# Second self-attention with one combined query-key matrix instead of two projections

## The chip, the cores and the metric

The kernel runs on one core of one Trainium2 chip. The metric is the device time of the program in microseconds. A matmul of f32 operands is shown in the trace as two MATMUL records and two weight loads; a transpose on TensorE is one.

## The reference

A decoder of two layers works on x of 4 batches, 1024 rows and 256 features. Layer 0 is a masked self-attention of 16 heads, a cross-attention and a quantised feed-forward with a depthwise convolution. Layer 1 is the self-attention that is changed here, a cross-attention and a gated feed-forward. After each of the six parts the input is added and a layer norm follows. The part that is changed has a single head of 256 features:

```python
def _L1_attn_ref(x, W_query, W_key, W_value):
    q = jnp.einsum('bnd,de->bne', x, W_query)
    k = jnp.einsum('bnd,de->bne', x, W_key)
    v = jnp.einsum('bnd,de->bne', x, W_value)
    sqrt_d = jnp.sqrt(jnp.asarray(OUT_DIM, dtype=jnp.float32))
    scores = jnp.einsum('bie,bje->bij', q, k) / sqrt_d
    attn = jax.nn.softmax(scores, axis=1)
    return jnp.einsum('bij,bie->bje', attn, v)
```

The softmax runs over the query index i, and the result has one row for each key index j. There is no bias in q and k.

## The kernel before, in words

The program has four stages, one after the other. The third, from L1950 to L2556, computes three things interleaved: the rest of the quantised feed-forward of layer 0 (its first layer and convolution for batches 2 and 3, its second layer for all four), the self-attention of layer 1 for all four batches, and the first loads and projections of the fourth stage. The order is written out by hand in a loop over steps `s` (9 to 49) that stands once in each engine's block; each engine works its list in order and waits on semaphores. Eight steps make one batch. In the code `e` is the batch whose feed-forward is finished, `m` is the place in its eight steps, and tile `s - 17` is the tile of 128 keys whose scores are made in step `s`.

- TensorE, of one step with both kinds of work: the scores of a tile (`scores`, L2083: 128 keys by 1024 queries into psA), a chunk of the first feed-forward layer (`first_layer`, L2072), the values of the tile before (`values`, L2094), and the transposes of the exponentials (`transpose_rows`, L2103).
- At `m` = 5 the second feed-forward layer (`second_layer`, L2119, eight tiles of 8 matmuls). At `m` = 6 the rows of the batch are transposed (`transpose_x`, L2124, four groups), and keys and queries of the first 512 rows are projected (`project_qk`, L2132: for each two chunks of 128 output features, each chunk two matmuls of 512 columns). At `m` = 7 keys and queries of the last 512 rows, and the first four tiles of `v` (`project_v`, L2139). The other four tiles of `v` come in the step after it. For batch 1 the transposes for the next first layer (`prepare`, L2065) follow at the end of the step `m` = 6.
- ScalarE copies every projection out of PSUM (`copy_xt` L2257, `copy_qk` L2264, `copy_v` L2271). Beside that it has the exponentials of the scores (L2235) and, for the feed-forward, Silu, Abs and two taps of the convolution.
- VectorE finds the maximum of each key tile's scores (L2448), adds the middle tap, rounds the hidden values (`hq`, L2488) and does residuals and norms. GpSimd adds the last tap (L2339), scales the hidden values (L2349) and rounds x for the next first layer (L2331, L2332).

All projections, `v` tiles, `values` and second-layer tiles share the two banks of psO in turn: `slot_c` (L2037) makes TensorE wait until the result before last has been read. `xt`, the transposed exponentials and some small spreads share the two banks of psB in the same way (`slot_t`, L2031). `number_c` fixes the turn of each result ahead. `XT3` holds the transposed rows of one batch, `ka` the keys of one batch, `qa` the queries of two. The trace calls `XT3` XT_sb, `wk_a1` wk_a_sb and `wq_a1` wq_a_sb.

Of the kernel before, what the change touches and what calls it, by code (L numbers as in the profile page):

```python
# [22 lines left out]
F32 = mybir.dt.float32  # L23
# [23 lines left out]
def decoder_kernel(nc, t, out):  # L47
# [21 lines left out]
    def sb(name, shape, dt=F32, ctx=top, side="left"):  # L69
        return ctx.enter_context(nc.sbuf_tensor(name + "_sb", shape, dt, side=side))  # L70
# [1478 lines left out]
    XR = sb("XR", [P, 2, NT, D], F32, third_stage)  # L1549
    XT3 = sb("XT3", [P, KC, S], F32, third_stage)  # L1550
    xq = sb("xq", [P, NT, D], BF16, f0_stage, "right")
# [7 lines left out]
    hq = sb("hq", [P, FH, S], BF16, f0_stage, "right")  # L1559
    qa = sb("qa", [P, 2, KC, S], F32, third_stage)  # L1560
    ka = sb("ka", [P, KC, S], F32, third_stage)
# [75 lines left out]
    for s in range(BEGIN, STEPS + 1):  # L1637
# [18 lines left out]
        if m in (6, 7) and e is not None:  # L1656
            if m == 6:
                for i in range(NT // 2):
                    number_t(("xt", e, i))
            for qk in ("k", "q"):  # L1660
                for c in range(KC):
                    number_c((qk, e, c, m - 6))
        if m == 7 and e is not None:
# [286 lines left out]
    with nc.Block() as block:  # L1950
        @block.sync
        def _(sp):
# [28 lines left out]
            load_xr(0)  # L1981
            for dst, name in ((wk_a1, "L1_attn_W_key"), (wq_a1, "L1_attn_W_query"), (wv_a1, "L1_attn_W_value")):
                sp.dma_start(dst[:, :, :], feature_rows(t[name])).then_inc(wa_loaded, 16)
# [46 lines left out]
        def _(pe):  # L2030
# [52 lines left out]
            def scores(a):  # L2083
                b, j = a // NT, a % NT
                if j == 0:
                    pe.wait_ge(c_act, C_FREED[("q", b, KC - 1, 1)])
                if a > 0:
                    pe.wait_ge(s_exped, a)
                for n in range(NC):
                    last = gemm(psA[:, 0, n * 512:(n + 1) * 512], lambda k: ka[:, k, j * P:(j + 1) * P],  # L2090
                                lambda k: qa[:, b % 2, k, n * 512:(n + 1) * 512], KC)
                last.then_inc(s_full, 1)
# [38 lines left out]

            def project_qk(qk, e, c, n):  # L2132
                w = wk_a1 if qk == "k" else wq_a1
                pe.wait_ge(t_act, T_FREED[("xt", e, 2 * n + 1)])
                k = slot_c((qk, e, c, n))
                gemm(psO[:, k, :], lambda i: w[:, i, c * P:(c + 1) * P], lambda i: XT3[:, i, n * 512:(n + 1) * 512],
                     KC).then_inc(c_full, 1)

            def project_v(e, j):  # L2139
                pe.wait_ge(t_act, T_FREED[("xt", e, j // 2)])  # L2140
                k = slot_c(("v", e, j))
                gemm(psO[:, k, 0:D], lambda i: XT3[:, i, j * P:(j + 1) * P], lambda i: wv_a1[:, i, :],
                     KC).then_inc(c_full, 1)
# [3 lines left out]
            for s in range(BEGIN, STEPS + 1):  # L2147
# [24 lines left out]
                if m in (6, 7) and e is not None:  # L2172
                    if m == 6 and e == 0:
                        pe.wait_ge(wa_loaded, 16 * 3)
                    if m == 6:
                        for i in range(NT // 2):
                            transpose_x(e, i)
                    for qk in ("k", "q"):
                        for c in range(KC):
                            project_qk(qk, e, c, m - 6)  # L2180
                if m == 7 and e is not None:
# [17 lines left out]
        def _(act):  # L2199
# [57 lines left out]
            def copy_xt(e, i):  # L2257
                key = ("xt", e, i)
                act.wait_ge(t_full, T_SLOT[key])
                nc.scalar.activation(XT3[:, :, 2 * i * P:2 * (i + 1) * P].rearrange("p c (n q) -> p n c q", n=2),  # L2260
                                     psB[:, t_bank(key), :].rearrange("p (n c q) -> p n c q", n=2, c=KC),
                                     ACT.Copy).then_inc(t_act, 1)
# [15 lines left out]
            for s in range(BEGIN, STEPS + 1):  # L2278
# [17 lines left out]
                if m in (6, 7) and e is not None:  # L2296
                    if m == 6:
                        for i in range(NT // 2):
                            copy_xt(e, i)
                    for qk in ("k", "q"):  # L2300
                        for c in range(KC):
                            copy_qk(qk, e, c, m - 6)
                if m == 7 and e is not None:
# [738 lines left out]
```

## Time and profile before

| | us |
|---|---|
| median of 3 runs | 2462.32 |
| lowest and highest run | 2461.2, 2466.6 |
| span of the profiled execution | 2470.6 |
| TensorE busy in the span | 2108.0 |
| VectorE, ScalarE, GpSimd busy | 1446.1, 1215.5, 767.3 |
| third stage in the profiled execution, about | 1521 to 2000 |

No time other than its span is given for the profiled execution; the span is 8.3 us above the median of the runs. An instruction's duration in the trace is longer than its share of the engine when instructions follow each other closely: eight records of a 128x512 f32 matmul are listed with 3.60 us, while the next group starts 3.43 us after them. The cost of a group on TensorE is therefore read from start to start.

### The profile page before, as it was taken

The page shows a single profiled execution, that of the slowest core. Times are in us where ns is not written, and L with a number is a line of the kernel's source. Part 1 is how long each engine was busy: PE and PEld are TensorE (multiplying, and loading weights), DVE is VectorE, ACT ScalarE, POOL GpSimd, SP SyncE. Part 2 cuts the span into 40 slices and gives each one's busy share as a digit, 9 for nine tenths or more (in the row PEclk, how much of TensorE's full clock was granted, in tenths as well). Part 3 has the DMA queues.
Part 4 walks back from the last instruction along what each step waited for, and adds up shares of the span by engine and source line. Part 5 has one row for each costly group of instructions (what it writes and reads, how often), then busy time and mean ns, then how long its engine had stood idle before and what let it go on. Part 6 is the DMA issues. An engine that isn't in the chain of part 4 may idle for free. (4 is left out here: it accounts for less than half of the span.)

```text
span 2470.6 us, 33295 instructions
## 1 busy us (share of the span) xinstructions
PE 2108.0 (85%) x11586; PEld 1180.7 (48%) x11586; DVE 1446.1 (59%) x2698; ACT 1215.5 (49%) x2773; POOL 767.3 (31%) x1082
## 2 busy tenths in 40 slices
PE   6778888888888869999999985889899977788886
PEld 3333344344343345565555554556566643445455
DVE  5565466455655146566787885494834344557555
ACT  2345534544444436565787771567642314354352
POOL 4250220221001020011454551384824222443333
PEclk8889999999999879999999998999999978899898
DMA  7425433343241020000110114010001156544321
GB/s 157 105 45 135 83 75 70 75 86 76 42 67 45 20 74 1 7 29 25 44 59 24 47 46 156 32 43 9 28 26 49 37 118 123 116 94 89 80 59 40
DMA packets 132520, 156.60 MB, mean 63 GB/s; under 512 B 36493, under 2 KB 102929, under 8 KB 132258
## 3 DMA queue, kind: packets, MB, share of 16 engines
q1 hardware_dynamic: 132354, 154.47, 26.2%
q8 instruction: 94, 1.54, 0.3%
q14 instruction: 72, 0.59, 0.1%
HBM read 107.55 MB, written 46.86 MB: 62 GB/s over the span
## 5 line engine op out<-in xcount | busy, mean ns | idle before, releaser
L530 ACT ACTIVATE pbuf_sb<-psB 128x512 f32<-128x512 f32 (+1 forms) x608 | 330.8, 573 | 343.5 <-PE psB L409 318.5
L716 DVE TENSOR_REDUCE negm_sb<-psA 128x1 f32<-128x768 f32 (+6 forms) x352 | 347.4, 1022 | 135.6 <-PE psA L397 132.9
L406 PE MATMUL psB<-qst_sb,kst_sb 99*128 99x512 bf16 (+3 forms) x768 | 237.0, 339 | 42.0 <-ACT pbuf_sb L530 34.1
L1257 ACT ACTIVATE pw_sb<-psA,nmx_sb 128x154 f32<-128x154 f32 x512 | 191.9, 389 | 133.5 <-DVE nmx_sb L1402 133.5
L395 PE MATMUL psA<-kst_sb,qst_sb 96*128 96x512 bf16 (+3 forms) x768 | 200.0, 339 | 40.9 <-DVE negm_sb L716 34.4
L423 PE MATMUL psO<-pbuf_sb,V_sb 128*32 128x512 f32 (+3 forms) x1536 | 170.3, 517 | 8.4 <-ACT OT_sb L516 7.1
L1402 DVE TENSOR_REDUCE nmx_sb<-psA 128x4 f32<-128x616 f32 x128 | 101.8, 796 | 125.3 <-PE psA L1026 125.0
L406 PEld LDWEIGHTS psB<-qst_sb,kst_sb 99*128 99x128 bf16 x768 | 75.2, 99 | 183.2 <-ACT pbuf_sb L530 145.9
L2801 ACT ACTIVATE pb_sb<-psB 128x512 f32<-128x512 f32 x160 | 92.8, 601 | 134.3 <-PE psB L2691 131.1
L2918 DVE TENSOR_REDUCE negm_sb<-psA 128x2 f32<-128x320 f32 x256 | 115.9, 480 | 70.8 <-PE psA L2681 66.1
L395 PEld LDWEIGHTS psA<-kst_sb,qst_sb 96*128 96x128 bf16 x768 | 60.9, 99 | 165.0 <-DVE negm_sb L716 100.7
L2681 PE MATMUL psA<-kst_sb,qst_sb 97*128 97x160 bf16 x512 | 83.2, 250 | 46.3 <-DVE negm_sb L2918 40.6
L2448 DVE TENSOR_REDUCE nma_sb<-psA 128x1 f32<-128x1024 f32 x32 | 39.1, 1222 | 140.8 <-PE psA L2045 140.8
L979 PE MATMUL psO<-XT_sb,wq_x_sb 128*128 128x512 f32 x256 | 121.4, 597 | 0.0
L567 POOL TENSOR_TENSOR OT_sb<-OT_sb,rden_sb 128x1024 f32<-128x1024 f32 x15 | 35.3, 2352 | 277.0 <-DMA rden_sb<-dens_dram 277.0
L979 PE MATMUL psO<-wo_x_sb,ox_sb 128*128 128x256 f32 x512 | 115.6, 379 | 1.7 <-DVE famw_sb L1488 0.9
L2045 PE MATMUL psO<-va_sb,pat_sb 128*128 128x256 f32 x512 | 115.9, 379 | 1.0 <-DVE pat_sb L2475 1.0
L2045 PE MATMUL psA<-qa_sb,ka_sb 128*128 128x512 f32 x256 | 116.7, 599 | 0.0
L553 POOL TENSOR_TENSOR q_sb<-q_sb,parts_sb 128x512 f32<-128x512 f32 x32 | 37.8, 1180 | 229.7 <-ACT parts_sb L510 229.4
L2045 PEld LDWEIGHTS psO<-va_sb,pat_sb 128*128 128x128 f32 x512 | 96.9, 190 | 22.6 <-issue 7.7
L397 PE MATMUL psA<-masku_sb,identb_sb 128*128 128x128 bf16 x512 | 107.6, 224 | 0.0
L1040 PE MATMUL psB<-ident_sb,pr_sb 128*128 128x128 f32 x512 | 83.6, 286 | 27.0 <-DVE pt_sb L1395 26.9
(308 smaller groups left out, 4580.6 us busy)
## 6 DMA issues: line engine op xcount, KB each, us to landing
qst_sb<-parts_dram SPq DMA_DIRECT2D x192, 128.0 KB, 4.6
rden_sb<-dens_dram SPq DMA_DIRECT2D x128, 128.0 KB, 2.7
parts_dram<-parts_sb SPq DMA_DIRECT2D x32, 384.0 KB, 2.8
kst_sb<-parts_dram SPq DMA_DIRECT2D x96, 128.0 KB, 7.3
x_dram<-X_sb SPq DMA_DIRECT2D x64, 128.0 KB, 1.7
y_dram<-yw_sb SPq DMA_DIRECT2D x16, 512.0 KB, 2.8
Y_sb<-y_dram SPq DMA_DIRECT2D x16, 512.0 KB, 9.3
parts_dram<-partsb_sb SPq DMA_DIRECT2D x16, 384.0 KB, 3.0
```

Source lines behind the costliest of these rows:

```text
L395: nc.tensor.matmul(psA[:, k, at + lo:at + hi], qst[0:QK_ROWS, gg % 3, h, j * P:(j + 1) * P], kst[0:QK_ROWS, gg % 3, h, lo:hi], start=True, ...
L397: last = nc.tensor.matmul(psA[:, k, at + w - P:at + w], identb[:, :], masku[:, :], start=False, stop=True)
L406: last = nc.tensor.matmul(psB[:, k, at:at + hi - lo], kst[0:MAX_ROWS, gg % 3, h, i * P:(i + 1) * P], qst[0:MAX_ROWS, gg % 3, h, lo:hi], st ...
L423: last = nc.tensor.matmul(psO[32 * h:32 * h + 32, c, lo - c * 512:hi - c * 512], V[:, b % 2, i, at:at + 32], pbuf[:, i % 2, h, lo:hi], sta ...
L530: nc.scalar.activation(pbuf[:, key % 2, heads[0]:heads[-1] + 1, lo:hi], psB[:, (nb.n - 1) % 2, 0:len(heads) * (hi - lo)] .rearrange("p (h ...
L716: nc.vector.tensor_reduce(out=negm[:, gg % 2, heads[0]:heads[-1] + 1, j], in_=psA[:, (na.n - 1) % 2, :].rearrange("p (h n) -> p h n", h=le ...
L979: last = nc.tensor.matmul(dst, lhsT(i), rhs(i), start=(i == 0), stop=(i == n - 1))
L1257: last = nc.scalar.activation(pw[:, m % 2, h, :], psA[:, m % 2, at:at + K], ACT.Exp, bias=nmx[:, m % 2, h:h + 1], accum_out=psx[:, m % 3, ...
L1402: nc.vector.tensor_reduce(out=nmx[:, m % 2, :].rearrange("p (b a) -> p a b", a=2), in_=psA[:, m % 2, :].rearrange("p (a n) -> p a n", a=2) ...
L2045: last = nc.tensor.matmul(dst, lhsT(i), rhs(i), start=(i == 0), stop=(i == n - 1))
L2801: nc.scalar.activation(pb1[:, v % 2, h, :], psB[:, (nb.n - 1) % 2, :], ACT.Exp).then_inc(b_free, 1)
L2918: nc.vector.tensor_reduce(out=negm1[:, gg % 2, 2 * half:2 * half + 2, j], in_=psA[:, 0, half * 512:half * 512 + 2 * KP].rearrange("p (a n) ...
```

## The change

The query and key weights are loaded transposed. Their product, 256 by 256, is made once, before the rows of batch 0 are transposed, and ScalarE copies it to `wqk` with the factor 1/16 (`D ** -0.5`). For each batch only one projection is made with it (`project_k`), and the scores multiply its result by the plain transposed rows `XT3`, which is now kept for two batches. `qa`, its projection and its copies are gone. Loads, with their sizes and their order, stay; only the names of the two arrays change.

```diff
-    XT3 = sb("XT3", [P, KC, S], F32, third_stage)
+    XT3 = sb("XT3", [P, 2, KC, S], F32, third_stage)
+    wqk = sb("wqk", [P, KC, D], F32, third_stage)
-    qa = sb("qa", [P, 2, KC, S], F32, third_stage)
...
-            for qk in ("k", "q"):
-                for c in range(KC):
-                    number_c((qk, e, c, m - 6))
+            if m == 6 and e == 0:
+                number_c(("wqk",))
+            for c in range(KC):
+                number_c(("k", e, c, m - 6))
...
             def scores(a):
...
-                    pe.wait_ge(c_act, C_FREED[("q", b, KC - 1, 1)])
+                    pe.wait_ge(c_act, C_FREED[("k", b, KC - 1, 1)])
...
-                                lambda k: qa[:, b % 2, k, n * 512:(n + 1) * 512], KC)
+                                lambda k: XT3[:, b % 2, k, n * 512:(n + 1) * 512], KC)
...
-            def project_qk(qk, e, c, n):
-                w = wk_a1 if qk == "k" else wq_a1
+            def combine_weights():
+                k = slot_c(("wqk",))
+                for c in range(KC):
+                    last = gemm(psO[:, k, c * D:(c + 1) * D], lambda i: wk_a1[:, i, c * P:(c + 1) * P], lambda i: wq_a1[:, i, :], KC)
+                last.then_inc(c_full, 1)
+
+            def project_k(e, c, n):
                 pe.wait_ge(t_act, T_FREED[("xt", e, 2 * n + 1)])
-                k = slot_c((qk, e, c, n))
-                gemm(psO[:, k, :], lambda i: w[:, i, c * P:(c + 1) * P], lambda i: XT3[:, i, n * 512:(n + 1) * 512],
+                pe.wait_ge(c_act, C_FREED[("wqk",)])
+                k = slot_c(("k", e, c, n))
+                gemm(psO[:, k, :], lambda i: wqk[:, i, c * P:(c + 1) * P], lambda i: XT3[:, e % 2, i, n * 512:(n + 1) * 512],
                      KC).then_inc(c_full, 1)
...
                     if m == 6 and e == 0:
                         pe.wait_ge(wa_loaded, 16 * 3)
+                        combine_weights()
...
-            def copy_qk(qk, e, c, n):
-                key = (qk, e, c, n)
+            def copy_weights():
+                key = ("wqk",)
                 act.wait_ge(c_full, C_SLOT[key])
-                dst = ka[:, c, n * 512:(n + 1) * 512] if qk == "k" else qa[:, e % 2, c, n * 512:(n + 1) * 512]
-                nc.scalar.activation(dst, psO[:, c_bank(key), :], ACT.Copy,
-                                     scale=1.0 if qk == "k" else D ** -0.5).then_inc(c_act, 1)
+                nc.scalar.activation(wqk[:, :, :].rearrange("p c n -> p (c n)"), psO[:, c_bank(key), :], ACT.Copy,
+                                     scale=D ** -0.5).then_inc(c_act, 1)
+
+            def copy_k(e, c, n):
+                key = ("k", e, c, n)
+                act.wait_ge(c_full, C_SLOT[key])
+                nc.scalar.activation(ka[:, c, n * 512:(n + 1) * 512], psO[:, c_bank(key), :], ACT.Copy).then_inc(c_act, 1)
```

On TensorE, at the start of the third stage's attention (batch 0, from the second feed-forward layer to the first scores), the order before is this; x4 here counts matmuls as the program issues them.

```order
L2045 MATMUL psO<-w2q_sb,hq_sb 128x256 x64
L2128 MATMUL psB<-ident_sb,XR_sb 128x128 x16
L2045 MATMUL psO<-XT_sb,wk_a_sb 128x512 x4
L2045 MATMUL psO<-XT_sb,wq_a_sb 128x512 x4
L2045 MATMUL psA<-xqT_sb,w1q_sb 128x512 x4
L2045 MATMUL psO<-XT_sb,wk_a_sb 128x512 x4
L2045 MATMUL psO<-XT_sb,wq_a_sb 128x512 x4
L2045 MATMUL psO<-wv_a_sb,XT_sb 128x256 x8
L2045 MATMUL psA<-qa_sb,ka_sb 128x512 x4
```

And this is the order of the change at the same place, where wqk_sb is the product of the two weights.

```order
L2046 MATMUL psO<-w2q_sb,hq_sb 128x256 x64
L2046 MATMUL psO<-wq_a_sb,wk_a_sb 128x256 x4
L2129 MATMUL psB<-ident_sb,XR_sb 128x128 x16
L2046 MATMUL psO<-XT_sb,wqk_sb 128x512 x4
L2046 MATMUL psA<-xqT_sb,w1q_sb 128x512 x4
L2046 MATMUL psO<-XT_sb,wqk_sb 128x512 x4
L2046 MATMUL psO<-wv_a_sb,XT_sb 128x256 x8
L2046 MATMUL psA<-XT_sb,ka_sb 128x512 x4
```

Both query projections are gone; four shorter matmuls stand between the second layer and the transposes of x.

On TensorE at batch 1, `m` = 6, where the transposes of the rounded rows (xq_sb) follow the projections, the order before is:

```order
L2128 MATMUL psB<-ident_sb,XR_sb 128x128 x16
L2045 MATMUL psO<-XT_sb,wk_a_sb 128x512 x4
L2045 MATMUL psO<-XT_sb,wq_a_sb 128x512 x4
L2053 MATMUL psB<-identb_sb,xq_sb 128x128 x16
L2061 MATMUL psB<-ident_sb,finvx_sb 128x128 x8
L2045 MATMUL psA<-qa_sb,ka_sb 128x512 x4
```

In the change it is:

```order
L2129 MATMUL psB<-ident_sb,XR_sb 128x128 x16
L2046 MATMUL psO<-XT_sb,wqk_sb 128x512 x4
L2054 MATMUL psB<-identb_sb,xq_sb 128x128 x16
L2062 MATMUL psB<-ident_sb,finvx_sb 128x128 x8
L2046 MATMUL psA<-XT_sb,ka_sb 128x512 x4
```

The transposes of xq_sb now come right behind the key projection.

## Rows read from the trace of the kernel before

**Rows 1.** Page: busy time of each engine in the whole span.
```profile
PE 2108.0 (85%) x11586; PEld 1180.7 (48%) x11586; DVE 1446.1 (59%) x2698; ACT 1215.5 (49%) x2773; POOL 767.3 (31%) x1082
```

**Rows 2.** Stretches: busy us by engine, TensorE clock granted, DMA share, GB/s.
```profile
core 0: us, PE busy (x) PEld busy (x) DVE busy (x) ACT busy (x) POOL busy (x), PEclk, DMA share, GB/s
1553.00:1576.50 23.50, 20.85 (x60) 10.40 (x59) 3.91 (x7) 9.25 (x16) 4.03 (x7) 0.93 0.00 0
1600.00:1650.00 50.00, 43.56 (x190) 28.16 (x190) 42.16 (x61) 39.11 (x41) 47.38 (x63) 0.93 0.16 50
1789.00:1996.00 207.00, 201.89 (x846) 136.28 (x845) 80.95 (x176) 68.94 (x115) 64.53 (x112) 1.00 0.16 43
```

**Rows 3.** Waits, 1550 to 2000 us: total us, times, longest.
```profile
DVE nma_sb L2448 <- PE psA L2045: 140.8, 23, 14.8
ACT pa_sb L2235 <- DVE nma_sb L2448: 105.2, 22, 13.8
```

**Rows 4.** Instructions of L2045: count, ns min/median/max, first and last start.
```profile
L2045 PE MATMUL psO<-XT_sb,wq_a_sb x64: 592/592/667, 1560.9 to 1910.8; 128*128 128x512 f32 x64
```

**Rows 5.** TensorE in order of time, batch 3: start us, length, group.
```profile
1893.19 3.60 PE L2045 MATMUL psO<-XT_sb,wq_a_sb 128*128 128x512 f32 x8
1896.62 3.60 PE L2045 MATMUL psA<-qa_sb,ka_sb 128*128 128x512 f32 x8
```

**Rows 6.** TensorE in order of time, batch 0, projections.
```profile
1555.29 0.66 PE L2128 MATMUL psB<-ident_sb,XR_sb 128*128 128x128 f32 x4 [1.89 <-DVE XR_sb L2509]
1555.78 5.29 PE L2045 MATMUL psO<-XT_sb,wk_a_sb 128*128 128x512 f32 x8
1560.91 3.60 PE L2045 MATMUL psO<-XT_sb,wq_a_sb 128*128 128x512 f32 x8
1564.35 1.03 PE L2045 MATMUL psA<-xqT_sb,w1q_sb 128*128 128x512 bf16 x4
1569.57 3.67 PE L2045 MATMUL psO<-XT_sb,wq_a_sb 128*128 128x512 f32 x8 [0.77 <-ACT ka_sb L2268]
1576.69 3.60 PE L2045 MATMUL psA<-qa_sb,ka_sb 128*128 128x512 f32 x8
```

**Rows 7.** VectorE and ScalarE, batch 0: residual of tile 6, first copy of x.
```profile
1551.24 0.48 DVE L2501 SCALAR_TENSOR_TENSOR XR_sb<-psO,finvy_sb,XR_sb 128x256 f32<-128x256 f32 x1
1552.00 1.09 ACT L2260 ACTIVATE XT_sb<-psB 128x512 f32<-128x512 f32 x2 [26.66 <-PE psB L2128]
```

**Rows 8.** TensorE, batch 1: v of 128x256 columns, then scores.
```profile
1695.11 3.77 PE L2045 MATMUL psO<-wv_a_sb,XT_sb 128*128 128x256 f32 x16
1698.71 3.60 PE L2045 MATMUL psA<-qa_sb,ka_sb 128*128 128x512 f32 x8
```

**Rows 9.** TensorE, batch 1, m = 6.
```profile
1672.38 3.60 PE L2045 MATMUL psO<-XT_sb,wq_a_sb 128*128 128x512 f32 x8
1675.81 1.06 PE L2053 MATMUL psB<-identb_sb,xq_sb 128*128 128x128 bf16 x16
1677.73 2.05 PE L2061 MATMUL psB<-ident_sb,finvx_sb 128*128 128x128 f32 x16 [0.86 <-ACT xqT_sb L2206]
1679.61 3.60 PE L2045 MATMUL psA<-qa_sb,ka_sb 128*128 128x512 f32 x8
```

**Rows 10.** GpSimd and ScalarE at the same place.
```profile
1673.02 0.85 POOL L2332 TENSOR_SCALAR xq_sb<-Xq_sb 128x256 bf16<-128x256 f32 x1
1676.50 2.06 ACT L2206 ACTIVATE xqT_sb<-psB 128x512 bf16<-128x512 bf16 x4
```

**Rows 11.** TensorE, batch 0: second-layer wait, scores after a wait.
```profile
1597.52 2.05 PE L2061 MATMUL psB<-ident_sb,fscy_sb 128*128 128x128 f32 x16 [1.04 <-DVE pat_sb L2475]
1626.80 1.26 PE L2107 MATMUL psB<-ident_sb,pa_sb 128*128 128x128 f32 x8 [2.23 <-ACT pa_sb L2235]
1627.85 5.17 PE L2045 MATMUL psA<-qa_sb,ka_sb 128*128 128x512 f32 x8
1632.86 1.03 PE L2045 MATMUL psA<-xqT_sb,w1q_sb 128*128 128x512 bf16 x4
1641.22 3.58 PE L2045 MATMUL psO<-w2q_sb,hq_sb 128*128 128x256 bf16 x16 [1.93 <-DVE hq_sb L2488]
```

**Rows 12.** GpSimd, batch 0 to 1: scaling of the hidden values, first and last of three groups.
```profile
1602.19 8.29 POOL L2349 TENSOR_TENSOR Y_sb<-Y_sb,rb_sb 128x256 f32<-128x256 f32 x12
1633.41 7.02 POOL L2349 TENSOR_TENSOR Y_sb<-Y_sb,rb_sb 128x256 f32<-128x256 f32 x8
```

More of the change, by code:

```diff
@@ L1981, in _ @@
             load_xr(0)
-            for dst, name in ((wk_a1, "L1_attn_W_key"), (wq_a1, "L1_attn_W_query"), (wv_a1, "L1_attn_W_value")):
+            for dst, name in ((wk_a1, "L1_attn_W_keyT"), (wq_a1, "L1_attn_W_queryT"), (wv_a1, "L1_attn_W_value")):
                 sp.dma_start(dst[:, :, :], feature_rows(t[name])).then_inc(wa_loaded, 16)
@@ L2141, in project_v @@
                 k = slot_c(("v", e, j))
-                gemm(psO[:, k, 0:D], lambda i: XT3[:, i, j * P:(j + 1) * P], lambda i: wv_a1[:, i, :],
+                gemm(psO[:, k, 0:D], lambda i: XT3[:, e % 2, i, j * P:(j + 1) * P], lambda i: wv_a1[:, i, :],
                      KC).then_inc(c_full, 1)
@@ L2177, in _ @@
                             transpose_x(e, i)
-                    for qk in ("k", "q"):
-                        for c in range(KC):
-                            project_qk(qk, e, c, m - 6)
+                    for c in range(KC):
+                        project_k(e, c, m - 6)
                 if m == 7 and e is not None:
@@ L2259, in copy_xt @@
                 act.wait_ge(t_full, T_SLOT[key])
-                nc.scalar.activation(XT3[:, :, 2 * i * P:2 * (i + 1) * P].rearrange("p c (n q) -> p n c q", n=2),
+                nc.scalar.activation(XT3[:, e % 2, :, 2 * i * P:2 * (i + 1) * P].rearrange("p c (n q) -> p n c q", n=2),
                                      psB[:, t_bank(key), :].rearrange("p (n c q) -> p n c q", n=2, c=KC),
                                      ACT.Copy).then_inc(t_act, 1)
-            def copy_qk(qk, e, c, n):
-                key = (qk, e, c, n)
+            def copy_weights():
+                key = ("wqk",)
                 act.wait_ge(c_full, C_SLOT[key])
-                dst = ka[:, c, n * 512:(n + 1) * 512] if qk == "k" else qa[:, e % 2, c, n * 512:(n + 1) * 512]
-                nc.scalar.activation(dst, psO[:, c_bank(key), :], ACT.Copy,
-                                     scale=1.0 if qk == "k" else D ** -0.5).then_inc(c_act, 1)
+                nc.scalar.activation(wqk[:, :, :].rearrange("p c n -> p (c n)"), psO[:, c_bank(key), :], ACT.Copy,
[4 more added lines that the diff above has]
+                nc.scalar.activation(ka[:, c, n * 512:(n + 1) * 512], psO[:, c_bank(key), :], ACT.Copy).then_inc(c_act, 1)
             def copy_v(e, j):
@@ L2296, in _ @@
                 if m in (6, 7) and e is not None:
+                    if m == 6 and e == 0:
+                        copy_weights()
                     if m == 6:
@@ L2299, in _ @@
                             copy_xt(e, i)
-                    for qk in ("k", "q"):
-                        for c in range(KC):
-                            copy_qk(qk, e, c, m - 6)
+                    for c in range(KC):
+                        copy_k(e, c, m - 6)
                 if m == 7 and e is not None:
@@ L3022 @@
         if name in ("L0_attn_w_in", "L0_attn_w_out", "L0_xattn_Wq", "L0_xattn_Wk", "L0_xattn_Wv", "L0_xattn_Wo",
-                    "L0_ffn_w1", "L0_ffn_w2", "L1_ffn_W_r", "L1_ffn_W_k", "L1_ffn_W_v"):
+                    "L0_ffn_w1", "L0_ffn_w2", "L1_ffn_W_r", "L1_ffn_W_k", "L1_ffn_W_v", "L1_attn_W_query", "L1_attn_W_key"):
             arrays[name + "T"] = np.ascontiguousarray(a.T)
```

## The prediction

> **What bounds the kernel now.** I read the page's busy times first, then the stretches, then the waits, then the engines in order of time around every projection. Over the whole span TensorE is the busiest engine by far, 2108.0 of 2470.6 us [rows 1]. That is an average over four stages, so the third stage is read by itself. From 1789 to 1996 us, where the projections of batches 2 and 3 lie, TensorE is busy 201.89 of 207 us at full granted clock; no other engine reaches 81 us [rows 2]. Around batch 0's and 1's feed-forward it is less clear: from 1600 to 1650 us TensorE is busy 43.56 of 50 us, GpSimd 47.38 and VectorE 42.16. The waits say who is late: the longest total is VectorE's wait for scores from TensorE, 140.8 us in 23 waits, and behind it ScalarE's wait for the maxima of those scores, 105.2 us [rows 3]. So TensorE work that stands ahead of scores delays them, except where another engine's chain reaches the same point later. The prediction is a walk over the eight places where a query projection stands, asking at each what TensorE finds when it comes 3.43 us earlier.
>
> **What goes.** 64 records of a 128x512 f32 matmul read the query weights [rows 4]: 4 batches x 2 halves of the rows x 4 matmuls x 2 records. In batch 3 eight of them start at 1893.19 and the scores behind them at 1896.62, so one group costs 3.43 us [rows 5], and eight groups 8 x 3.43 = 27.4 us. The 16 copies on ScalarE go too; I count them at nothing, since in 1789 to 1996 us ScalarE is busy 68.94 of 207 us.
>
> **What comes.** The product of the weights is four matmuls of 256 columns, eight records. Sixteen such records take 1698.71 - 1695.11 = 3.60 us with the waits for their copies [rows 8], so eight take 1.8. They stand after the second layer of batch 0 and before the transposes of x, where TensorE later sits idle 1.89 us until VectorE has normalised the last rows [rows 6]. The product's bank is that of the second layer's tile 6, which VectorE reads at 1551.24 to 1551.72 [rows 7]. So it runs from about 1551.8 to 1553.5. The first eight transposes of x then run about 1553.5 to 1554.4. ScalarE, which starts the x copies at 1552.00 today and needs 0.55 us for each [rows 7], first copies the product, about 1553.7 to 1554.3, then the first two groups until about 1555.4. The last transposes, which start at 1555.29 today, need the second of these copies (same bank), so they start about 1555.4, and the key projection about 1555.9 instead of 1555.78. That is 0.15 us lost: the cover is the 1.89 us wait. If there were no cover, the price would be the 1.8 us and one copy of 0.6, 2.4 in all. The new wait of `project_k` on the copy of the product is met at about 1554.3, before the rows are ready, and is free in all later batches. The loads of the weights are the same in size and place, and the wait for them was already there.
>
> **Batch 0, first half, and the clock.** The key projection of this half takes 1560.91 - 1555.78 = 5.13 us, not 3.43 [rows 6]; the granted clock in this stretch is 0.93 [rows 2], so part of the group ran at 1.2 GHz and the rest at 2.4. Before it fell TensorE had stood idle 1.89 us with a few short transposes around. With the change this gap is filled by the product. Bounds for the effect: nothing (5.13 stays), or 5.13 - 3.43 = 1.7 us gained. I take 1.7, since the activity before the fall is what the change adds to; the other end stays in the range.
>
> The Trainium skill, "TensorE: Matmul & The Clock Gate", part 1, says that the throttled clock is the default and that activity of TensorE releases it, while idle time brings it back. By that rule the filled gap gains the 1.7 us; without it the sum would be 1.7 us smaller. The same rule speaks against the change elsewhere, since it makes TensorE less busy; this is the last rival below.
>
> **Batch 0, second half.** TensorE waits 0.77 us for the copy of the first key chunk, because ScalarE is in the convolution taps [rows 6]. After the change it is the first `v` tile that needs this same bank, at the same distance from the first-layer group that releases the taps. So the wait stays at 0.77 us and the full 3.43 us go. Batch 0 gives 2 x 3.43 - 0.15 + 1.7 = 8.4 us, seen as first scores at about 1568.3 instead of 1576.69 [rows 6].
>
> **Batch 1, first half.** Here something else is late next. The transposes of xq follow the projections, at 1675.81 [rows 9], and the last xq tile is ready on GpSimd at 1673.02 + 0.85 = 1673.87 [rows 10]. With the query group gone TensorE comes at 1672.38. The first eight transposes (tiles 0 to 3) run at once, the last eight wait until 1673.9 and end about 1674.4. ScalarE copies each half in 1.03 us (2.06 for both [rows 10]); the second half's copy ends about 1675.6, and the last spread group, about 0.9 us long, can start only then. Scores start about 1676.5 instead of 1679.61: 3.1 us gained, 0.3 lost. If GpSimd were later by a microsecond relative to TensorE, a microsecond more would be lost, so I bound this place by 1 and 3.43.
>
> **The other places.** Batch 1, second half: 3.43. Batch 2 and 3, both halves: TensorE goes from the projection to scores or to `v` without any idle time [rows 2, 5], and the two copies left end before the next user of their bank, as they do now: 4 x 3.43 = 13.7.
>
> **Later work** moves as a whole. The GpSimd chain that ends in the rounding for which TensorE waits 1.93 us at 1641.22 starts behind the scale spreads of TensorE at 1597.52 [rows 11, 12], so it comes earlier with them. The fourth stage's loads are issued ahead of batch 3's projections; 6.9 us less stand between them and their first use.
>
> **Sum.** 8.4 + 3.1 + 3.43 + 13.7 = 28.6 us. The profiled span would go from 2470.6 to 2442.0. The runs' median is 8.3 us below that span, so the gain is taken from the median: 2462.3 - 28.6 = 2433.7 us. Own bounds: at best everything, 27.4 + 1.7 = 29.1; at worst no clock gain, an uncovered product (2.4) and 1 us only at batch 1: 27.4 - 2.4 - 2.4 = 22.6. With some 2 us for the spread of the runs (2461.2 to 2466.6), and one more at the low end for a fall of the clock elsewhere that may vanish, that is 2430 to 2442.
>
> **Rivals.**
> 1. The GpSimd chain takes the gain of the first two batches. From 1600 to 1650 us GpSimd is 95% busy [rows 2], and the scaling runs from 1602.19 to 1640.43 with other work between [rows 12]. If its start were set by data or by its own queue, and not by the spreads, the 8.4 and 6.5 us of batches 0 and 1 would turn into longer waits at 1641.22 and its counterpart. Left are 13.7 us: 2448.6. Against it: the scaling reads the spread scales that TensorE makes at 1597.52, and those stand behind batch 0's projections in TensorE's own order.
> 2. Copies become late. With half as many matmuls between results, each of the eight halves could meet the 0.77 us wait that one shows now [rows 6]: 7 x 0.77 = 5.4 us less, 2439. Against it: `v` tiles come only after both key chunks, and a chunk takes 1.7 us against a copy of 0.6.
> 3. Slower: the clock. After an idle of 2.23 us the scores at 1627.85 took 5.01 us to the next group instead of 3.43 [rows 11], 1.58 us for one fall to 1.2 GHz. TensorE loses 27 us of dense work in this stage and keeps its waits, so such falls could become more frequent. They decide from 28.6 / 1.58 = 18 further falls on; 22 would make it 6 us slower, 2468. Against it: the stretch where half of the removed groups lie has clock 1.00 and stays without gaps.
>
> By the rule on the clock gate in the Trainium skill, named above, more idle time lowers the clock; the trace agrees for the fall at 1627.85, 1.58 us.
>
> **Chances.** Forecast (2430 to 2437) 0.70; the copies or a later GpSimd at batch 1 (2437 to 2443) 0.14; the GpSimd chain (2443 to 2455) 0.08; nothing gained, by a mixture that I can't name 0.03; slower by the clock 0.05. The first two hold 0.84, so the range is 2430 to 2442. A difference under 0.2%, 4.9 us, can't be told from none. Faster 0.92, same 0.03, slower 0.05.
>
> **What would show it.** No records of the query group, 64 fewer, and eight new ones of 128x256 at the start. First scores of batch 0 about 8.4 us earlier, at 1568.3, and the key group there with 3.4 to 3.6 us (right on the clock) or about 5.1 (wrong). At batch 1 a wait of about 1 us of the xq transposes for xq_sb. Batches 2 and 3 shorter by 6.9 us each with no new wait. VectorE's total wait for scores smaller by some 27 us. It would be wrong if TensorE's waits for hq_sb (1.93 us) grew by several microseconds, if waits for ka_sb stood before each `v` group, or if the granted clock of the stage's second half fell below 1.00.

## The result, and the profile after

| | before | changed |
|---|---|---|
| median of the first comparison, us | 2463.55 (2461.2 to 2466.6, 4 runs) | 2445.99 (2445.07 to 2447.15, 4 runs) |
| ratio, 95% interval | | 0.9924 (0.991 to 0.9938) |
| all executions of the study: mean and its standard error | 2468.1, 0.6 (93 runs) | 2445.2, 1.2 (13 runs) |
| all executions: median, lowest, highest | 2467.5, 2450.9, 2481.2 | 2445.4, 2436.9, 2452.3 |
| span of the first profile | 2470.6 | 2445.4 |

The changed kernel is 17.6 us faster in the first comparison, where 28.6 were forecast and a time of 2430 to 2442 us. Over all executions, which were taken on several occasions and chips, it is 22.9 +- 1.3 us faster. So the direction was right and the size was not. The third stage gave what was forecast, as the next part shows. Of the shortfall about half comes from which executions of the kernel before were compared, and about half was lost outside the third stage.

The 93 executions leave out one, e3, which is told of below. `+-` is one standard error throughout, worked out as if the executions were independent.

Page of the changed kernel, busy time of each engine; it answers to [rows 1]:

```profile
PE 2085.8 (85%) x11503; PEld 1174.1 (48%) x11530; DVE 1449.0 (59%) x2698; ACT 1206.4 (49%) x2758; POOL 767.8 (31%) x1082
```

TensorE is listed with 22.3 us less, and its share of the span is unchanged. The program has 56 matmul records fewer (64 gone, 8 new), as the weight loads show (11586 to 11530); the page lists 83 fewer, so some 27 records are missing from this trace and the busy time is only roughly comparable.

**The third stage.** TensorE in order of time, changed kernel, batch 0; it answers to [rows 6, 7]. Columns: start, length, group, and in brackets the idle time ahead and who ended it.

```profile
1554.49 1.96 PE L2046 MATMUL psO<-wq_a_sb,wk_a_sb 128*128 128x256 f32 x8 [0.34 <-DVE XR_sb L2513]
1556.29 1.04 PE L2129 MATMUL psB<-ident_sb,XR_sb 128*128 128x128 f32 x8
1557.72 1.12 PE L2129 MATMUL psB<-ident_sb,XR_sb 128*128 128x128 f32 x8 [0.39 <-ACT XT_sb L2267]
1558.67 3.60 PE L2046 MATMUL psO<-XT_sb,wqk_sb 128*128 128x512 f32 x8
...
1562.97 3.60 PE L2046 MATMUL psO<-XT_sb,wqk_sb 128*128 128x512 f32 x8
1567.34 3.69 PE L2046 MATMUL psO<-wv_a_sb,XT_sb 128*128 128x256 f32 x16 [0.77 <-ACT ka_sb L2280]
1570.87 3.60 PE L2046 MATMUL psA<-XT_sb,ka_sb 128*128 128x512 f32 x8
```

The product starts at 1554.49 and the transposes that had waited 1.89 us now wait 0.39 us, for a copy. The key group is listed with 3.60 us where it had 5.29 before. From start to start it took 5.13 before and 3.66 now (1558.67 to 1562.33); here the first of four records of the next group is missing, and the profiles that have it give 3.44. The wait of 0.77 us for the key copy is there, ahead of `v`. First scores come 27.70 us after the first second-layer matmul (1543.17 to 1570.87), where they came 36.28 after it before (1540.41 to 1576.69): 8.6 us, predicted 8.4.

Batch 1, first half, TensorE; it answers to [rows 9]:

```profile
1663.52 3.90 PE L2046 MATMUL psO<-XT_sb,wqk_sb 128*128 128x512 f32 x8
1667.25 0.61 PE L2054 MATMUL psB<-identb_sb,xq_sb 128*128 128x128 bf16 x8
1668.19 0.62 PE L2054 MATMUL psB<-identb_sb,xq_sb 128*128 128x128 bf16 x8 [0.33 <-POOL xq_sb L2344]
1669.17 2.05 PE L2062 MATMUL psB<-ident_sb,finvx_sb 128*128 128x128 f32 x16 [0.36 <-ACT xqT_sb L2213]
1671.06 3.60 PE L2046 MATMUL psA<-XT_sb,ka_sb 128*128 128x512 f32 x8
```

And GpSimd at the same place, answering to [rows 10]:

```profile
1667.29 0.85 POOL L2344 TENSOR_SCALAR xq_sb<-Xq_sb 128x256 bf16<-128x256 f32 x1
```

The last eight transposes wait 0.33 us for the xq tile that ends at 1668.14. From the key group to the scores before, 10.67 us; now 7.54: 3.13 gained, predicted 3.1. That the two agree so closely is in part luck: the xq tile was ready 4.62 us after the start of the key group and not 4.93 as before, and from there to the scores it took 2.92 us and not the 2.6 of the forecast.

Batch 3, TensorE, second half of the projections; it answers to [rows 5]:

```profile
1882.12 3.60 PE L2046 MATMUL psO<-XT_sb,wqk_sb 128*128 128x512 f32 x8
1885.55 3.77 PE L2046 MATMUL psO<-wv_a_sb,XT_sb 128*128 128x256 f32 x16
1889.16 3.60 PE L2046 MATMUL psA<-XT_sb,ka_sb 128*128 128x512 f32 x8
```

And stretches of the changed kernel, answering to [rows 2] (the same parts of the program for the second and third row there), with the fourth stage:

```profile
core 0: us, PE busy (x) PEld busy (x) DVE busy (x) ACT busy (x) POOL busy (x), PEclk, DMA share, GB/s
1777.00:1970.00 193.00, 187.88 (x812) 129.97 (x811) 80.93 (x176) 64.18 (x107) 64.49 (x112) 1.00 0.17 47
1594.00:1640.00 46.00, 38.64 (x161) 25.16 (x162) 38.23 (x50) 36.40 (x39) 44.82 (x56) 0.93 0.17 55
1976.00:2445.00 469.00, 378.78 (x1888) 215.34 (x1888) 262.62 (x655) 185.62 (x333) 169.14 (x277) 0.89 0.42 90
```

The stretch without gaps is 14 us shorter for the same work but the projections (193 against 207), still at clock 1.00. Waits of the changed kernel, 1550 to 1974 us; they answer to [rows 3]:

```profile
DVE nma_sb L2460 <- PE psA L2046: 117.3, 23, 12.0
ACT pa_sb L2242 <- DVE nma_sb L2460: 105.2, 22, 13.8
```

VectorE's wait for scores fell by 23.5 us (some 27 were forecast); ScalarE's wait behind it is the same 105.2. Two of the prediction's signs of being wrong are read from TensorE's own waits in the same stretch. Before, for the rounded hidden values:

```profile
PE psO L2045 <- DVE hq_sb L2488: 3.8, 2, 1.9
```

In the changed kernel, for them and for the key copies:

```profile
PE psO L2046 <- DVE hq_sb L2500: 3.8, 2, 1.9
PE psO L2046 <- ACT ka_sb L2280: 0.8, 1, 0.8
```

The waits for hq_sb did not grow, and of the waits for ka_sb there is only the one.

The gain place by place, from the start times of the same groups in both profiles:

| place | gained, us | predicted |
|---|---|---|
| batch 0, both halves and the clock | 8.58 | 8.4 |
| batch 1, first half | 3.13 | 3.1 |
| batch 1, second half | 3.44 | 3.43 |
| batches 2 and 3, four halves | 3.43, 3.44, 3.42, 3.44 | 4 x 3.43 |
| between them | -0.4 | 0 |
| third stage | 28.45 | 28.6 |

The 0.4 us are lost just ahead of batch 1's key projection, and there the clock is lower: from 1655 to 1670 us of the changed kernel the granted clock is 0.77, at the same place before (1661 to 1676) 0.89.

**The rest.** From the first scores of the fourth stage on, before took 2470.6 - 2001.87 = 468.7 us and the changed kernel 2445.4 - 1976.18 = 469.2. Ahead of the first second-layer matmul they took 1540.4 and 1543.2. These two parts, which no edit touches, are where the rest of the story is.

### The profile page after: what moved, and what is told of

Its sections match the earlier page's. It is cut to its first block and busy times, and to the rows that moved or that the text cites. A ratio compares the mean times of both kernels' runs of the same rounds, so it can differ in the third digit from the quotient of the medians.

```text
span 2445.4 us, 33126 instructions
## 1 busy us (share of the span) xinstructions
PE 2085.8 (85%) x11503; PEld 1174.1 (48%) x11530; DVE 1449.0 (59%) x2698; ACT 1206.4 (49%) x2758; POOL 767.8 (31%) x1082
## 5 line engine op out<-in xcount | busy, mean ns | idle before, releaser
L2046 PE MATMUL psA<-XT_sb,ka_sb 128*128 128x512 f32 x256 | 116.0, 596 | 0.0
L1040 PE MATMUL psB<-ident_sb,pr_sb 128*128 128x128 f32 x512 | 83.6, 286 | 27.1 <-DVE pt_sb L1395 26.9
```

The source lines that it names most:

```text
L2046: last = nc.tensor.matmul(dst, lhsT(i), rhs(i), start=(i == 0), stop=(i == n - 1))
```

## The experiments

All the profiles of the study are cut in the same three parts: the time until the first matmul of the second layer (L2122), from there to the first scores of the fourth stage (here the third stage), and the rest. "First scores" is their distance from the first second-layer matmul.

| profile | first part | third stage | fourth | first scores |
|---|---|---|---|---|
| before | 1540.4 | 461.5 | 468.7 | 36.3 |
| e1, before | 1531.9 | 463.1 | 466.8 | 36.2 |
| e13, before | 1539.0 | 461.7 | 472.0 | 36.3 |
| e14, before | 1538.9 | 463.0 | 470.2 | 36.2 |
| e10, before, other arrays | 1539.0 | 461.4 | 468.6 | 36.2 |
| e9, before with the product | 1536.7 | 460.9 | 472.6 | 34.8 |
| changed | 1543.2 | 433.0 | 469.2 | 27.7 |
| e2, changed | 1537.7 | 433.1 | 472.8 | 27.8 |
| e4, changed | 1543.7 | 433.0 | 472.9 | 27.7 |
| e15, changed | 1536.5 | 432.8 | 470.0 | 27.8 |
| e16, changed | 1536.7 | 432.4 | 472.0 | 27.3 |
| e8, changed without the product | 1543.3 | 434.4 | 471.8 | 29.2 |
| e5, e6, e7, changed with a delay | 1549.9, 1542.5, 1540.6 | 433.5, 434.5, 435.2 | 469.1, 465.3, 471.1 | 27.6, 27.8, 27.8 |
| e11, projections twice, batches 0, 1 | 1542.7 | 445.0 | 467.8 | 33.7 |
| e12, projections twice, batches 2, 3 | 1537.1 | 446.7 | 466.6 | 27.8 |

### Both kernels again (e1 to e4, e13 to e16)

Edit: none. The question was why the profiles were 25 us apart and the timed runs 17.6.

> The kernel before, unchanged, run again to see how its executions spread and where the profiled one lay. Theory A (the profiled execution of before was an unusually long one, its span of 2470.6 us stands 7 to 9 us above its other runs): spans here lie near 2462 us, and the new profile shows where the 8 us of difference were: in the granted clock of stages 1, 2 or 4 or in the third stage. Theory B (the four runs of before happened to be short): spans here spread from 2460 to 2471 and the median is nearer to 2468.

> The changed kernel, unchanged, timed in more rounds. Theory A: ratio again 0.991 to 0.994, time 2446 us. Theory B: the ratio moves to about 0.9885, a gain of 28 us, since the third stage alone is 28 us shorter in the two profiles at hand.

> The kernel before once more, for a third profile. Theory A: span near 2462 us, the third stage from its first second-layer matmul to the first scores of the fourth stage shorter than the 461.5 us of the first profile, or the other stages shorter by 8 us. Theory B: span anywhere from 2460 to 2471.

> The changed kernel once more, for a third profile. Both theories: span 2443 to 2446 us; the third stage from its first second-layer matmul to the first scores of the fourth stage 433 us as in the first profile, if the third stage hardly varies.

Measured: e1 2471.15 us median (2463.09 to 2479.5, 12 runs) against 2467.52 for 17 further runs of the same kernel, ratio 1.0012 (0.9996 to 1.0028). e2 2444.54 (2436.91 to 2452.31, 6 runs), ratio 0.9907 (0.9886 to 0.9927). e4 2451.35. e3 had a mean granted clock of 0.729 and took 2830.9 us; even in its third stage (1757 to 2309 us), where the first two profiles come to 0.97, it was 0.75. Neither theory had it, and nothing is read of the change from it.

Theory A falls: the profiled execution of before was not unusual. Before spreads from 2451 to 2481 us, and the four runs of the first comparison lay 4.6 us under the mean of all 93. Theory B is right in kind, but hardly in size: the ratio went to 0.9907, which is 23 us, and its interval, 18 to 28 us, just misses B's 0.9885. e4's span of 2449.6 us lay above the 2443 to 2446 expected, its third stage at the expected 433.0. So 6 us were still missing: 29.2 in the third stage (means 462.1 and 432.9 of five profiles each, e10 counted as before), 22.9 +- 1.3 in all. This sets a difference of ten profiles against one of 106 executions, and the profiled ones need not be typical.

One place of spread is seen by laying e1 beside the first profile. TensorE, before, first stage, at the key tile behind the first maxima:

```profile
177.40 0.82 PE L395 MATMUL psA<-kst_sb,qst_sb 96*128 96x512 bf16 x2 [10.45 <-DVE negm_sb L716]
```

The same instruction in e1:

```profile
166.03 0.82 PE L395 MATMUL psA<-kst_sb,qst_sb 96*128 96x512 bf16 x2 [4.42 <-DVE negm_sb L716]
```

The wait is 4.4 to 4.8 us in some executions and 8.3 to 10.6 in the others (10.07 in the first profile of the changed kernel), for one and the same program; e3 is left out. It was short in 2 of 6 profiles of before (e9, e10 counted) and in 2 of 11 of the others. It doesn't fix the length of the first part by itself: e10 has a short one (4.51) and a first part of 1539.0 us, e15 a long one (10.56) and 1536.5.

Is the missing 6 us chance? With e13 to e16 more profiles were taken.

> Another profile of the kernel before. Over all its executions so far the changed kernel is 22.3 us shorter, though its third stage is 28.4 shorter in every profile; 6 us are lost outside the third stage. Theory I (a wait of TensorE in the first stage, 4.4 or about 10 us long, and the fourth stage's length, 466 to 473 us, fall out by chance, and fell worse for the changed kernel in both): first second-layer matmul 1532 to 1544 us, fourth stage 466 to 473, no difference in the means of the two kernels over more profiles. Theory J (the changed kernel really is later): before starts the second layer at 1532 to 1540, the changed kernel at 1540 to 1545.

> As for the run before it: one more profile of the kernel before. Theory J has its first second-layer matmul at or before 1540 us and its fourth stage at 467 to 469 us, theory I at any value between 1532 and 1550, and 466 to 473.

> One more profile of the changed kernel. Third stage 433.0 us again. Theory J: first second-layer matmul 1540 us or later and a fourth stage of 469 to 473 us; theory I: any value between 1532 and 1550, and 465 to 473.

> As for the run before it: third stage 433.0 us; by theory J the first second-layer matmul at 1540 us or later and 469 to 473 us for the fourth stage, by theory I any value.

Measured: 2474.42, 2473.95, 2441.07 and 2442.84 us. Theory J falls in its sharp form: the changed kernel's first part ended at 1536.5 and 1536.7 us, under the 1540 that it required, and the fourth stages of e13 and e14, 472.0 and 470.2, lie above the 467 to 469 that it required of before. The means of five profiles each are 1537.8 and 1539.6 for the first part, 469.3 and 471.4 for the fourth stage. That is 1.7 and 2.1 us more for the changed kernel, each from values that scatter over 4 to 9 us, so chance is not excluded for either. The 6.3 +- 1.4 us are more than chance; that the profiles locate 3.8 of them in these two parts is an indication and no more. The other 2.5 are not in the profiles at all: by their spans the two kernels are 25.5 us apart (2469.2 and 2443.8 in the mean of five).

**The clock of the timed executions.** Each execution is recorded with its span and mean granted clock, except the four timed runs of before in the first comparison. In every profile but e3's the granted clock is 0.5 (1.2 GHz) or 1 (2.4 GHz) at any time, so twice its shortfall from 1, times the span, is the time at 1.2 GHz. From these rows:

| executions | number | mean granted clock | at 1.2 GHz, us | time, us |
|---|---|---|---|---|
| before | 89 | 0.9483 | 255.1 +- 1.6 | 2468.3 |
| before with the product (e9), with other arrays (e10) | 24 | 0.9482 | 255.2 +- 2.3 | 2467.1 |
| changed, projections twice (e11, e12) | 20 | 0.9467 | 261.2 +- 3.4 | 2454.6 |
| changed with a delay (e5 to e7) | 33 | 0.9461 | 263.8 +- 2.3 | 2447.3 |
| changed | 13 | 0.9455 | 266.1 +- 2.9 | 2445.2 |

The changed kernel spends 11.1 +- 3.3 us more at 1.2 GHz. The same holds on each occasion by itself: in the executions taken together with e1 to e4 it is 270.2 against 259.4 us, and with e5 to e7 263.8 against 253.3. Nor is it arithmetic: 28.6 us less at full clock alone would leave the mean at 0.9477. Among the 89 executions of before, each further microsecond at 1.2 GHz goes with 0.37 us of time, and 255.1 and 266.1 us then differ by 4.1 us. At the same time at 1.2 GHz the changed kernel is 27.1 +- 0.9 us faster. So about 4 of the missing 6 us go together with more time at the lower clock. Whether the clock makes the time or a longer wait makes both is not shown, and where it happens isn't either: the five profiles of the changed kernel have 261 us at 1.2 GHz in the mean, those of before 265.

### A delay ahead of the fourth stage (e5 to e7)

```diff
             def normalise(a):
                 dve.wait_ge(arstd_ready, a + 1)
+                if a == NT * B - 1:
+                    for _ in range(1):   # 2 in e6, 3 in e7
+                        link(nc.vector.tensor_copy(XT3[:, 0, 1, :], XT3[:, 0, 0, :]))
```

> The changed kernel with one VectorE copy of 1024 elements (about 0.7 us) put between the last norm's wait and the last norm of the third stage, so that the fourth stage starts 0.7 us later after the same third stage. Theory C (what the fourth stage takes depends on where its start falls against the rhythm in which the granted clock changes; the changed kernel's three profiles all start it at one such place and take 469.2, 472.8, 472.9 us from the first scores on, those of before start at two others and take 468.7 and 466.8): the fourth stage changes by 1 to 5 us for a delay of 0.7, downwards if it meets the places of before. Theory D (the fourth stage's time has nothing to do with its start; the changed program has it longer by 3 us for its code or data placement, or by chance): fourth stage 469 to 473 us as without the delay, total 0.7 us longer.

> The same with two such copies, about 1.4 us. Theory C: the fourth stage again another length, between 466 and 473 us, always the same one in the profile and other stretches of 1.2 GHz than without the delay. Theory D: 469 to 473 us, total 1.4 us longer.

> The same with three such copies, about 2.2 us. Theory C: near the second profile of before, whose fourth stage took 466.8 us, so 466 to 468 us and a total not above the changed kernel's 2445.9. Theory D: 469 to 473 us, total 2.2 us longer.

Measured: 2446.55 us (2438.61 to 2454.81, 12 runs), 2448.84 (2443.68 to 2451.73, 9 runs) and 2447.77 (2438.95 to 2457.93, 12 runs); ratios 0.9909, 0.9930, 0.9925. Fourth stages 469.1, 465.3 and 471.1 us. Neither theory came out clean: e5 doesn't tell them apart, since its 469.1 lies in the range of D and also below two of the three lengths without a delay by 4 us; e6 fits neither; e7 misses the 466 to 468 of C and fits D. The delays changed the third stage by 0.5, 1.5 and 2.2 us, and the totals by 0.6 to 2.9, as a mere delay would. But the fourth stage of the changed kernel without any delay takes 469.2 to 472.9, and the delayed ones reach 465.3, below any of before, so a long fourth stage is no fixed property of the changed program. The fourth stage of e6 as one stretch; columns: start and end, length, busy time and instructions of each engine, granted clock, DMA share and what was moved in GB/s:

```profile
1977.00:2442.00 465.00, 375.90 (x1888) 214.08 (x1888) 262.45 (x655) 185.42 (x333) 169.13 (x277) 0.89 0.42 91
```

The same stretch of the program in e2, the changed kernel without a delay:

```profile
1971.00:2443.00 472.00, 378.25 (x1888) 215.12 (x1886) 263.27 (x655) 185.91 (x333) 168.77 (x277) 0.89 0.42 89
```

TensorE is busy 375.90 us of 465 and 378.25 us of 472, at the same mean clock to two digits, 0.89. So of the 7 us between them 2.35 are busy time and 4.65 are waiting (89.1 against 93.75 us). What selects the one or the other length was not found and stays open.

### Without the product, and the product alone (e8, e9)

```diff
                         pe.wait_ge(wa_loaded, 16 * 3)
-                        combine_weights()
...
-                gemm(psO[:, k, :], lambda i: wqk[:, i, c * P:(c + 1) * P], ...
+                gemm(psO[:, k, :], lambda i: wk_a1[:, i, c * P:(c + 1) * P], ...
```

Without the product its copy, its turn of the psO banks and the waits for it are gone too.

> The changed kernel without the product of the weights: keys are projected with the key weights as loaded, so the scores are not those of the reference; nothing else differs. If the product's only effects are those of the prediction (0.15 us lost behind the 1.89 us wait, 1.7 us won because the clock stays at 2.4 GHz): the key group of batch 0 takes about 5.1 us again, and first scores come about 1.5 us later after the first second-layer matmul than the 27.7 us of the changed kernel, 29.2 us. If the clock's better place in the changed kernel has another cause, the key group stays at 3.4 us and first scores come at 27.5 us.

TensorE, e8, the key group of batch 0 and the transposes ahead of it:

```profile
1558.11 0.72 PE L2127 MATMUL psB<-ident_sb,XR_sb 128*128 128x128 f32 x4 [1.89 <-DVE XR_sb L2515]
1558.63 5.26 PE L2044 MATMUL psO<-XT_sb,wk_a_sb 128*128 128x512 f32 x8
1563.73 1.03 PE L2044 MATMUL psA<-xqT_sb,w1q_sb 128*128 128x512 bf16 x4
```

The wait of 1.89 us is back, the key group takes 5.10 us, and first scores come at 29.2 us, as the sum had it. From 1558 to 1565 us the granted clock of e8 is 0.76, from 1558 to 1563 us of the changed kernel 1.00. One execution, 2451.27 us.

e9 adds the same product and its copy to the kernel before, used by nothing:

```diff
                     if m == 6 and e == 0:
                         pe.wait_ge(wa_loaded, 16 * 3)
+                        combine_weights()
```

> The kernel before with the product of the weights and its copy added, and used by nothing; both projections stay. If the product costs nothing behind the 1.89 us wait and keeps the clock at 2.4 GHz, the key group of batch 0 takes 3.4 us instead of 5.1, first scores come 34.8 us after the first second-layer matmul instead of 36.3, and the third stage is 460.0 instead of 461.5 us; the total 1 to 2 us under before, within its uncertainty. If the product costs its 1.8 us and its copy, the third stage is 463 us.

TensorE, e9, batch 0:

```profile
1548.18 1.97 PE L2048 MATMUL psO<-wq_a_sb,wk_a_sb 128*128 128x256 f32 x8 [0.34 <-DVE XR_sb L2519]
...
1552.37 3.60 PE L2048 MATMUL psO<-XT_sb,wk_a_sb 128*128 128x512 f32 x8
1555.80 3.60 PE L2048 MATMUL psO<-XT_sb,wq_a_sb 128*128 128x512 f32 x8
```

The product's eight records take 1.80 us, and the key group behind them 3.43 instead of 5.13. First scores come 34.8 us after the second layer's start instead of 36.3. Eight matmul records more make this place 1.5 us shorter. All profiles agree: in the six without the product the key group took 5.10 to 5.13 us, in the eleven with it 3.44 (3.65 where the next group's first record is missing). The third stage is 460.9 us where 460.0 were expected; the four profiles of before scatter from 461.5 to 463.1. In the total it is not to be seen: 2467.23 us (2461.85 to 2472.17, 12 runs), ratio 0.9999 (0.9984 to 1.0015).

### The arrays alone (e10)

```diff
-            for dst, name in ((wk_a1, "L1_attn_W_key"), (wq_a1, "L1_attn_W_query"), ...
+            for dst, name in ((wk_a1, "L1_attn_W_keyT"), (wq_a1, "L1_attn_W_queryT"), ...
```

> The kernel before with the query and key weights given transposed, so that its scores are not those of the reference; all instructions are the same. Theory E (the other arrays in memory, or their places, make the first two stages of the changed kernel 3 to 5 us longer): the first second-layer matmul starts at 1540 us or later, the total is 3 to 5 us above before. Theory F (the first two stages differ by chance only): total within 2 us of before, ratio 1.000.

Measured: 2468.03 us (2459.39 to 2473.23, 12 runs), ratio 0.9998 (0.9981 to 1.0014), first part 1539.0. Theory E falls; the arrays are not the source of the missing 6 us, as far as the kernel before can show it.

### The removed time given back (e11, e12)

```diff
                 k = slot_c(("k", e, c, n))
+                if e < 2:   # e >= 2 in e12
+                    gemm(psO[:, k, :], lambda i: wqk[:, i, c * P:(c + 1) * P], ..., KC)
                 gemm(psO[:, k, :], lambda i: wqk[:, i, c * P:(c + 1) * P], ..., KC).then_inc(c_full, 1)
```

> The changed kernel with every key projection of batches 0 and 1 made twice into the same place, so that eight matmul records a half are there as before, without their copies. By the prediction's sum for these places the third stage is 433.0 + 2 x 3.43 (batch 0) + 3.1 + 3.43 (batch 1) = 446.4 us. If the GpSimd chain hid part of the gain of these batches, the third stage grows by less than 13.4 us. Total 2459 us if the rest of the program is unmoved; with the lesser slope of the runs so far (23 us for 28) 2457.

> The same for batches 2 and 3. By the prediction's sum 433.0 + 4 x 3.43 = 446.7 us for the third stage, with no wait taking part of it. Total 2459.5 us if the rest of the program is unmoved; 2457 with the lesser slope.

TensorE, e11, batch 0, second half:

```profile
1565.95 7.03 PE L2046 MATMUL psO<-XT_sb,wqk_sb 128*128 128x512 f32 x16
1572.82 3.77 PE L2046 MATMUL psO<-wv_a_sb,XT_sb 128*128 128x256 f32 x16
```

TensorE, e11, batch 1, first half:

```profile
1668.53 7.03 PE L2046 MATMUL psO<-XT_sb,wqk_sb 128*128 128x512 f32 x16
1675.40 1.06 PE L2054 MATMUL psB<-identb_sb,xq_sb 128*128 128x128 bf16 x16
```

In e12 the third stage is 446.7 us, to 0.1 us what the sum gives. In e11 it is 445.0 and not 446.4, and less than the expected growth was named there as the sign of a hidden gain. The 1.4 us have another source: in batch 0 the doubled group stands between the taps and the `v` tile and covers the 0.77 us wait, and ahead of batch 1's key projection the granted clock was higher (0.89 from 1660 to 1676 us, where the changed kernel has 0.77 at that place), which is worth the 0.4 us of the table of gains. Some 0.2 us stay unaccounted for. So the four removed groups of batches 0 and 1 were on the path: with the unchanged waits for hq_sb and the place-by-place gains, rival 1 falls. Totals: 2455.06 us (2444.39 to 2464.78, 12 runs), ratio 0.9955 (0.9935 to 0.9974), and 2454.39 (2448.06 to 2461.43, 8 runs), ratio 0.9956 (0.9936 to 0.9975). Against the changed kernel's mean of 2445.2 +- 1.2 us the means are 2454.6 +- 2.1 and 2454.7 +- 1.7: 9.4 +- 2.4 and 9.5 +- 2.1 us for 12.0 and 13.7 us in the third stage. The first lies one error short of the full amount, the second two. The totals also lie under the 2459 and 2459.5 us expected for an unmoved rest and nearer to the 2457 of the lesser slope. So half of the removed work given back costs at least most of its time, but whether all of it reaches the end isn't settled by these two runs. The time at 1.2 GHz, 261.2 us, lies between the 266.1 of the changed kernel and the 255.1 of before.

## Why the prediction was wrong, point by point

- **TensorE bounds the third stage, and each group costs 3.43 us.** Right. Five places gave 3.42 to 3.44, batch 1's first half the predicted 3.1, and batch 0's two halves with the clock 8.6 for 8.4 (the key group began 0.13 us later, forecast 0.15).
- **The product is hidden, and keeps the clock up in batch 0.** Right, shown from both sides by e8 (taken away: 5.10 us for the key group) and e9 (added to before: 3.43). The rule of the Trainium skill, "TensorE: Matmul & The Clock Gate", part 1, that activity of TensorE releases the throttled clock and idle time brings it back, agrees with both. About 0.15 us of batch 0's gain stay unexplained (8.58 for 8.4).
- **The next user of the bank waits 0.77 us as before.** Right. Rival 2, copies late at the other places, did not occur.
- **At batch 1 the rounding of x is late next.** Right in place; the wait was 0.33 us and not about 1, since the key group itself took 3.73 us (granted clock 0.77 around it) and the transposes of x ahead of it 3.60 us from start to start and not 3.32.
- **Sum of the third stage, 28.6.** 28.45 between the first two profiles and 29.2 between the means of five each.
- **"Later work moves as a whole", and the gain is taken from the median of three runs.** These are the two steps that failed. The forecast of 2433.7 us was 12.3 too low. Of these, 5.8 are the baseline: it took three runs of before (median 2462.3) for the kernel's time, and their spread of 5 us for the spread of the measurement. Over 93 runs the mean is 2468.1 and the range 30 us. Another 5.7 (28.6 - 22.9) is gain that didn't reach the end of the program, a term that the sum put at nothing; 0.8 is that the four runs of the changed kernel lay over its mean. Seen as a gain, 28.6 against 17.6, the 11.0 are 4.6 + 0.8 + 5.7, rounded. The span of the profile stood 8.3 us above the median of the runs; I noted it and used the lower number.
- **The rest of the difference.** With the third stage as measured, 6.3 +- 1.4 us were lost outside it (29.2 - 22.9). Neither the arrays (e10) nor the product (e9) cost anything that could be measured in the kernel before, and a chain on GpSimd doesn't hide the gain in the stage. What goes with the loss is the granted clock: 11.1 +- 3.3 us more at 1.2 GHz, which by the executions of before stand for about 4 us. Profiles put 1.7 us in the first part and 2.1 us in the fourth stage, neither clear of chance, and don't show the longer time at 1.2 GHz. The cause stays open. Why a program that differs only later should have a later first part does too; the different length of the program's instruction stream was not varied by itself.
- **Rival 3, the clock.** It came true in part, and I had it with the wrong sign in the range, where a microsecond at the low end stood for a fall of the clock that may vanish. In the third stage it cost nothing but the 0.4 us ahead of batch 1: in the stretch where half of the removed groups lie the granted clock stayed at 1.00. Over the whole program the mean is 0.9455 against 0.9483, and the loss that goes with it is about 4 us, far from the 28.6 at which the rival would decide.

Measured against its own mean of all executions, 2468.1 - 28.6 = 2439.5 would have been forecast and 2445.2 was measured.

## What to carry to other kernels

Where one engine has no gaps, the cost of a removed group is its start-to-start time, and the sum over the places holds to 0.6 us in the stage (28.6 forecast, 28.45 and 29.2 measured). What the whole program shows is that sum plus whatever its untouched stages do, and here whole runs scatter by 13 to 17 us to either side of their mean: before a few tenths of a per cent are forecast, compare the span of the profile with the runs, and widen the range by their distance. Look at the recorded clock of every execution too, and not only at that of the profile: here it showed a difference between the kernels that ten profiles didn't. An idle gap of TensorE next to dense work can be worth filling with useful matmuls for the clock alone; here 1.80 us of them, in a gap of 1.89, made the place 1.5 us shorter, which the total was too coarse to show.

## What was not expected of the hardware

- The same program with the same data takes 2450.9 to 2481.2 us over 93 executions, 1.2%. One wait of TensorE in the first stage falls out at 4.4 to 4.8 us or at 8.3 to 10.6, and the fourth stage takes 465 to 473 us over all profiles but that of e3.
- The changed kernel has less dense work of TensorE and a lower mean granted clock, 0.9455 +- 0.0006 over 13 executions against 0.9483 +- 0.0003 over 89, and more time at 1.2 GHz in absolute terms, 266.1 against 255.1 us.
- Eight more records of matmul (1.80 us) made batch 0's start 1.5 us shorter in e9, since the key group behind them took 3.43 us, its time at full granted clock (2.4 GHz), and not 5.13.
- One execution in the study, e3, had a mean granted clock of 0.729, with 0.75 in the dense third stage, and took 2830.9 us. Kernel and data were those of e1.
